# Top-k routing and experts of the last layer: ranking laid out over both halves of the partitions, and the chosen expert's product by masked features summed in PSUM

## The chip, the cores and the metric

The kernel runs on one core of one Trainium2 chip, as a single launch. The metric is the device time of that core in microseconds, as a median of several runs.

## The reference, cut to what matters

Four adaLN layers, each an attention and a feed-forward block, work on x of shape 8 x 256 x 128 in float32. The change lies in the last block alone: layer 3's mixture of 8 experts. With `h` the normalised and modulated x, and `gb` the block's gate vector per batch (sign times the larger of |g| and 0.25):

```python
# EPS = 1e-06, SINKHORN_ITERS = 8
t = jnp.log(jnp.clip(h @ gate_w, EPS))          # 8 batches x 256 tokens x 8 experts
for _ in range(8):
    t = t - logsumexp(t, axis=-2, keepdims=True)   # over the tokens
    t = t - logsumexp(t, axis=-1, keepdims=True)   # over the experts
gates = jnp.exp(t)
gv, idx = jax.lax.top_k(jnp.swapaxes(gates, -1, -2), m)   # m = 256 // 8 = 32 tokens for each expert
hard_gates = (gv > 0.5)
out = einsum(h[idx], experts) * hard_gates
y = zeros.at[idx].set(out)                      # .set: of several slots of a token, the last written stays
x = x + gb * y
```

So each of the 64 pairs of a batch and an expert takes its 32 best tokens. A token that several experts took gets the product of only one: the one with the latest slot, where the slot's order is rank first, then expert. For that the kernel needs each taken token's rank, and ties between equal gates are ordered by token, as top_k does.

## The kernel before, in words

x stays in SBUF as 16 tiles of 128 tokens x 128 dimensions (8 batches, 2 tiles each). Each engine has its own list of instructions, written out by hand in order, and engines meet only at semaphores. On DVE nearly every step of the routing goes through `then`, which makes the engine wait for the step's own completion before the next one. What runs in the last block, in order:

- `wide_front("l3_ffn")`: layer norm of all 16 tiles at once. DVE first copies silu(c) spread over 128 columns (L1838) for eight matmuls on PE (L991) that give the gate vector of each batch on all partitions. Then statistics, a power on POOL (L968), normalised tiles, transposes on PE (L997), scale and shift on ScalarE into `feats` (features of each batch, dimension on the partition, L3096), and the logits (L1003).
- `l3_ffn`: clip into `routes` (L2952), which also releases POOL's `partition_all_reduce` (L972). Then `wide_gates` on DVE (L1861 to L1867) makes the gate vectors, and then DVE waits for POOL's maximum (`sink_max`) ahead of L2973.
- `l3_route`: rescaling, then 8 rounds (`ROUNDS3`) of Sinkhorn without logarithms. Each is a sum over tokens by a matmul with ones on PE (L1689), and five small DVE steps (L2979 to L2983).
- Ranking: the gates are transposed to 64 partitions (batch and expert) x 256 tokens (L1693, L2989), three rows are filled (L2990 to L2992), and four rounds of MAX8 and MATCH_REPLACE8 give the 32 largest values in order (L2995, L2996). A loop over all 32 of them (L3001 to L3004) then runs four instructions for each value: how many of the top values a gate is below, where it equals the value, a running count of these, and a predicated copy of that count.
- The key (rank x 8 + expert) is transposed back (L1698) and seven small DVE steps (L3014 to L3020) leave a mask, tokens x experts, with a 1 for the winning expert.
- `l3_out`, once for each of 4 pairs of batches, in a hardware loop: PE multiplies a pair's features by all 8 experts (L1710, two halves of four matmuls of 128x512), and DVE adds the eight results of a tile, each weighted by its mask column (L3036, L3038: 64 instructions of 128x128 in a pair). Then DVE multiplies by the gate vector (L2754) and adds to x (L2756). PE's first half of the next pair waits for DVE's copy of the features, the second for x.
- SP waits for the last pair and stores all of x in one DMA of 1024 KB (L680).

Of the kernel before, what the change touches and what calls it, by code (L numbers as in the profile page):

```python
# [7 lines left out]
BF16 = mybir.dt.bfloat16  # L8
I32 = mybir.dt.int32
# [103 lines left out]
DVE_STEPS = {"l1_ffn": 4, "l2_ffn": 3, "l3_attn": 1, "l3_out": 36}  # L113
# [56 lines left out]
def adaln_program(nc, x_in, c_in, const_in, ali_in, weights_in, out):  # L170
    ctx = ExitStack()
    with ctx:
# [144 lines left out]
        best = sb("best", [P, T * B])  # L317
        ps = ctx.enter_context(nc.psum_tensor("bank", [P, 8, 512], F32))
# [86 lines left out]
        wide_silu = wide_signal("wide_silu", **dict.fromkeys(wide, 1))  # L405
        wide_mod = wide_signal("wide_mod", **dict.fromkeys(wide, 2))
# [8 lines left out]
        pair_ready = signal("pair_ready", l1_ffn=1, l2_ffn=1, l3_out=1)  # L415
# [14 lines left out]
        out_psum = signal("out_psum", l1_attn=1, l2_ffn=1, l3_attn=1)  # L430
# [41 lines left out]
        hid_ready = signal("hid_ready", l0_ffn=E0 * 2, l1_ffn=EA, l2_ffn=O2)  # L472
        silu_g = signal("silu_g", l1_ffn=EA)
        expert_psum = signal("expert_psum", l0_ffn=E0, l1_ffn=EA, l3_out=2)
# [11 lines left out]
        out_taken = signal("out_taken", l1_attn=1, l3_attn=1)  # L486
# [19 lines left out]
        routes_ready = once("routes_ready")  # L506
# [98 lines left out]
        def _(sp):  # L605
# [73 lines left out]
            sp.wait_ge(pass_done.sem, sum(PASSES.values()) + 1)  # L679
            sp.dma_start(out.rearrange("b (t p) d -> p (b t) d", p=P), x[:]).then_inc(stored, 16)  # L680
            sp.wait_ge(stored, 16)

        @block.gpsimd
        def _(pool):
# [270 lines left out]
            for ph in WEIGHED:  # L955
# [13 lines left out]
                if ph == "l3_ffn":  # L969

                    pool.wait_ge(routes_ready, 1)
                    nc.gpsimd.partition_all_reduce(colmax[:], routes[:].rearrange("p t b e -> p (t b e)"), P,  # L972
                                                   bass.bass_isa.ReduceOp.max).then_inc(sink_max, 1)


        @block.tensor
        def _(pe):
            mm = nc.tensor.matmul

            def wide_front(ph, logits):  # L980
# [4 lines left out]
                for j in range(2):  # L985
# [3 lines left out]
                pe.wait_ge(wide_silu.sem, wide_silu(ph, 0, 1))  # L989
                for b in range(B):  # L990
                    last = mm(pb[6 + b // 4][:, b % 4 * D:(b % 4 + 1) * D], silu_8[:, b, :], W(ph, "wmod")[:, 2 * D:3 * D],  # L991
                              start=True, stop=True)
                last.then_inc(wide_mod.sem, 1)
# [690 lines left out]
            def l3_route():  # L1684
# [7 lines left out]
                for t in range(T):  # L1692
                    last = nc.tensor.transpose(pb[1][0:B * E3, t * P:(t + 1) * P], routes[:, t].rearrange("p b e -> p (b e)"), C("ident"))  # L1693
                last.then_inc(sink_sum, 1)
                pe.wait_ge(sink_next, ROUNDS3 + 2)
                n = B * E3
                for t in range(T):
                    last = nc.tensor.transpose(pb[0][:, t * n:(t + 1) * n], qT[0:n, 2, t * P:(t + 1) * P], C("ident", n)[:, 0:n])  # L1698
                last.then_inc(sink_sum, 1)

            def l3_out(p, ph="l3_out"):

                pe.wait_ge(pair_ready.sem, pair_ready(ph, p, 1))
                for r in range(2):
                    if r:

                        pe.wait_ge(pass_done.sem, pass_done(ph, p, 1))
                    for t in range(T):
                        for j in range(2):
                            last = mm(pb[4 * r + 2 * t + j][:], pair_feat[:, (r * T + t) * P:(r * T + t + 1) * P],  # L1710
                                      W("l3_ffn", "experts")[:, j * 512:(j + 1) * 512], start=True, stop=True)
                    last.then_inc(expert_psum.sem, 1)
# [29 lines left out]
            with pe.Fori(0, PAIRS) as p:  # L1742
                l3_out(p)
# [3 lines left out]
        def _(dve):  # L1747
# [85 lines left out]
            def wide_front(ph):  # L1833
# [4 lines left out]
                V_.tensor_copy(silu_8, silu_c[:, layer * B:(layer + 1) * B].unsqueeze(2).to_broadcast([P, B, P])).then_inc(wide_silu.sem, 1)  # L1838
# [10 lines left out]
                V_.tensor_scalar(scale_8, pb[0][:, B:2 * B], 1.0, None, ALU.add).then_inc(wide_scaled.sem, 1)  # L1849
                dve.wait_ge(wide_rstd_ready.sem, wide_rstd_ready(ph, 0, 1))  # L1850
# [1098 lines left out]
            def l3_ffn(ph="l3_ffn"):  # L2949
# [4 lines left out]
                wide_gates(ph)  # L2954
# [3 lines left out]
            def l3_route():  # L2958
# [11 lines left out]
                over_e = lambda v: v.unsqueeze(2).to_broadcast([P, T * B, E3])  # L2970
                dve.wait_ge(routes_ready, 1)
# [5 lines left out]
                for r in range(ROUNDS3):  # L2977
                    dve.wait_ge(sink_sum, r + 1)
# [4 lines left out]
                    V_.tensor_tensor(rows, rows, over_e(best[:]), ALU.mult).then_inc(sink_next, 1)  # L2983

                R = B * E3
                gate, work, key, strict, seen, same, run, one = (qT[0:R, i, :] for i in range(8))
                top = small[9][0:R, 0:M3]
                dve.wait_ge(sink_sum, ROUNDS3 + 1)
                then(V_.tensor_copy(gate, pb[1][0:R, 0:S]))  # L2989
# [18 lines left out]
                then(V_.tensor_scalar(strict, strict, float(E3), -float(E3), ALU.mult, ALU.add))  # L3008
                V_.scalar_tensor_tensor(key, strict, C("expert1", R), same, ALU.add, ALU.mult).then_inc(sink_next, 1)
# [4 lines left out]
                then(V_.tensor_copy(masks3[:].rearrange("p t b e -> p (t b e)"), pb[0][:, 0:T * R]))  # L3014
                then(V_.tensor_reduce(best[:], keys, AX.X, ALU.max))
                then(V_.tensor_tensor(won, keys, over_e(best[:]), ALU.is_equal))
                then(V_.tensor_scalar(keys, keys, 0.0, None, ALU.is_gt))
                then(V_.tensor_tensor(won, won, keys, ALU.mult))
                then(V_.tensor_scalar(rows, rows, 0.5, None, ALU.is_gt))
                then(V_.tensor_tensor(keys, won, rows, ALU.mult))  # L3020

            def l3_out(p, following, ph="l3_out"):
                count[0] = 0
                dve.wait_ge(pass_done.sem, pass_done(ph, p, 1))
                step(V_.memset(gap[:], 0.0))
                chosen = small[0][:, 0:2 * T * E3].rearrange("p (t b e) -> p t b e", t=T, b=2)
                step(V_.tensor_copy(chosen, masks3[:, :, bass.ds(p * 2, 2), :]))
                settle(ph, p)
                for r in range(2):
                    dve.wait_ge(expert_psum.sem, expert_psum(ph, p, r + 1))  # L3030
# [549 lines left out]
```

## Time and profile before

| | us |
|---|---|
| median of 3 runs (2676.94 to 2680.75) | 2680.1 |
| the profiled execution's own time | 2681.6 |
| its span, first to last instruction | 2679.8 |
| PE busy in the span | 2004.3 (75%) |
| DVE busy | 1739.8 (65%) |
| ScalarE busy | 1144.0 (43%) |
| POOL busy | 880.6 (33%) |

The device time is the span and 1.8 us around it. The rows below are from the same profiled execution. Times are from the start of the span, so the last block is what lies after about 2489 us. "PEclk" is the clock that TensorE was granted, as a share of 2.4 GHz: 0.50 is the lower of its two levels, 1.2 GHz.

### The profile page before, as it was taken

The page shows a single profiled execution, that of the slowest core. Times are in us where ns is not written, and L with a number is a line of the kernel's source. Part 1 is how long each engine was busy: PE and PEld are TensorE (multiplying, and loading weights), DVE is VectorE, ACT ScalarE, POOL GpSimd, SP SyncE. Part 2 cuts the span into 40 slices and gives each one's busy share as a digit, 9 for nine tenths or more (in the row PEclk, how much of TensorE's full clock was granted, in tenths as well). Part 3 has the DMA queues.
Part 4 walks back from the last instruction along what each step waited for, and adds up shares of the span by engine and source line. Part 5 has one row for each costly group of instructions (what it writes and reads, how often), then busy time and mean ns, then how long its engine had stood idle before and what let it go on. Part 6 is the DMA issues. An engine that isn't in the chain of part 4 may idle for free.

```text
span 2679.8 us, 44272 instructions
## 1 busy us (share of the span) xinstructions
PE 2004.3 (75%) x14672; PEld 1405.8 (52%) x14672; DVE 1739.8 (65%) x5467; ACT 1144.0 (43%) x3362; POOL 880.6 (33%) x1155
## 2 busy tenths in 40 slices
PE   3878989964477766775769999957757999999405
PEld 2445666651356555564746666634433666666302
DVE  5777353245888888888656666657654666664597
ACT  1443333419677777776112222213422655656000
POOL 3433121033545765556500000024200555555000
PEclk9887889975555555555569999978967999999558
DMA  3111000020000000000010000011110000000000
GB/s 110 44 42 40 17 20 28 2 84 21 7 13 13 7 13 8 13 1 1 1 44 1 0 0 0 0 28 48 40 61 11 1 1 1 1 1 1 0 0 16
DMA packets 57761, 49.60 MB, mean 19 GB/s; under 512 B 7000, under 2 KB 55864, under 8 KB 57016
## 3 DMA queue, kind: packets, MB, share of 16 engines
q1 hardware_dynamic: 54500, 45.53, 5.3%
q10 hardware_dynamic: 3040, 1.38, 0.3%
q8 instruction: 107, 1.75, 0.3%
q14 instruction: 114, 0.93, 0.1%
HBM read 19.78 MB, written 1.05 MB: 8 GB/s over the span
## 4 chain that ended last, share of the span: by engine, by line
PE 42%; DVE 30%; issue 8%; ACT 8%; SPq 5%; POOL 5%; ACTq 1%; DMA 1%; DVEq 0%; POOLq 0%
PE bank L1526 5%; PE bank L1518 5%; PE bank L1519 5%; SPq L556 4%; DVE weights L2484 4%; PE bank L1595 3%; PE bank L1248 3%; ACT rope_c L3262 2%; ACT rope_s L3262 2%; PE bank L1264 2%; PE bank L1632 2%; PE bank L1644 2%; DVE small L2522 2%; DVE feat_o L2534 1%; POOL big L706 1%
## 5 line engine op out<-in xcount | busy, mean ns | idle before, releaser
L1432 PE MATMUL bank<-V,probsT 128*128 128x9 f32 x1024 | 236.1, 364 | 76.7 <-ACT probsT L3273 76.7
L1432 PEld LDWEIGHTS bank<-V,probsT 128*128 128x128 f32 x1024 | 226.2, 329 | 114.1 <-ACT probsT L3273 94.5
L2129 DVE TENSOR_REDUCE nmax<-bank 128x4 f32<-128x1024 f32 x144 | 176.1, 1223 | 81.3 <-PE bank L1064 81.2
L3328 ACT ACTIVATE hid<-bank 128x512 f32<-128x512 f32 x144 | 85.7, 597 | 283.7 <-PE bank L1519 272.6
L1526 PEld LDWEIGHTS bank<-weights,hid 128*128 128x128 f32 x1152 | 151.2, 193 | 78.7 <-issue 75.5
L2718 DVE TENSOR_TENSOR hid<-hid,bank 128x512 f32<-128x512 f32 x144 | 98.7, 688 | 127.6 <-PE bank L1526 123.4
L1526 PE MATMUL bank<-weights,hid 128*128 128x128 f32 x1152 | 152.5, 277 | 12.5 <-DVE hid L2718 10.1
L3273 ACT ACTIVATE probsT<-bank 128x512 f32<-128x512 f32 x128 | 76.0, 597 | 179.8 <-PE bank L1419 177.4
L1518 PE MATMUL bank<-O,weights 128*128 128x512 f32 x288 | 150.3, 604 | 2.6 <-DVE big L2658 2.6
L1519 PE MATMUL bank<-O,weights 128*128 128x512 f32 x288 | 148.9, 599 | 0.0
L2732 DVE SCALAR_TENSOR_TENSOR O<-bank,O 128x128 f32<-128x128 f32 x496 | 138.9, 343 | 0.0
L793 POOL MEMSET big<- 128x4096 bf16 x1 | 3.5, 3512 | 411.9 <-DVE x L2756 411.9
L2903 DVE TENSOR_TENSOR kT<-bank,weights 128x256 f32<-128x256 f32 x128 | 54.1, 422 | 123.0 <-PE bank L1595 122.9
L706 POOL TENSOR_TENSOR big<-big,rinv 128x512 f32<-128x512 f32 x128 | 131.6, 1049 | 4.0 <-DVE rinv L2896 4.0
L3362 ACT ACTIVATE big<-bank,nmax 128x256 f32<-128x256 f32 x256 | 118.4, 472 | 16.7 <-DVE nmax L2891 16.7
L3108 ACT ACTIVATE feat_o<-bank 128x1024 f32<-128x1024 f32 x72 | 73.7, 1023 | 114.1 <-PE bank L1090 84.5
L3108 ACT ACTIVATE O<-bank 128x1024 f32<-128x1024 f32 x72 | 73.7, 1023 | 112.7 <-PE bank L1090 84.9
L2411 DVE TENSOR_REDUCE nmax<-bank 128x2 f32<-128x512 f32 x128 | 84.9, 683 | 34.1 <-PE bank L1406 34.1
L1406 PE MATMUL bank<-qT 48*128 48x256 bf16 x256 | 70.7, 405 | 45.7 <-ACT weights L3216 33.3
L2891 DVE TENSOR_REDUCE nmax<-bank 128x2 f32<-128x512 f32 x128 | 82.3, 684 | 30.6 <-PE bank L1606 30.6
L1519 PEld LDWEIGHTS bank<-O,weights 128*128 128x128 f32 x288 | 55.7, 193 | 70.5 <-issue 70.5
L1632 PE MATMUL bank<-const,big 128*128 128x128 f32 x512 | 83.1, 285 | 12.2 <-POOL big L706 10.4
(622 smaller groups left out, 5564.7 us busy)
## 6 DMA issues: line engine op xcount, KB each, us to landing
qT<-parts SPq DMA_DIRECT2D x276, 32.0 KB
big<-V SPq DMA_DIRECT2D x192, 32.0 KB
big<-parts SPq DMA_DIRECT2D x180, 32.0 KB
weights<-in_weights_l_ffn SPq DMA_DIRECT2D x1, 4832.0 KB, 14.4
weights<-in_weights_l_attn SPq DMA_DIRECT2D x1, 3904.0 KB, 12.5
weights<-in_weights_l_ffn SPq DMA_DIRECT2D x1, 3628.0 KB, 12.8
qT<-V SPq DMA_DIRECT2D x96, 32.0 KB
weights<-in_weights_l_ffn SPq DMA_DIRECT2D x1, 2304.0 KB, 7.8
```

What stands on the lines that cost most here:

```text
L556: queue.dma_start(stacks[m % STACKS][to, u * HALF:(u + 1) * HALF], pair_of(m, at, *of)).then_inc(stack_in[u].sem, 16)
L706: nc.gpsimd.tensor_tensor(row, row, rinv[:, h % H, :].unsqueeze(2).to_broadcast([P, T, S]), ALU.mult).then_inc(scaled.sem, 1)
L1432: last = mm(pb[1][:, t * S + h * wide:t * S + (h + 1) * wide], probsT[:, h % 2, at:at + P], values_of(b, k)[:, h * wide:(h + 1) * wide], s ...
L1518: mm(pb[two][:], W(ph, "gate")[:, cols], pair_feat, start=True, stop=True)
L1519: mm(pb[two + 1][:], W(ph, "up")[:, cols], pair_feat, start=True, stop=True).then_inc(hid_psum.sem, 1)
L1526: last = mm(pb[6 + e % 2][:, j * D:(j + 1) * D], risen(e)[:, j * P:(j + 1) * P], W(ph, "down")[:, e * D:(e + 1) * D], start=True, stop=True)
L1632: last = nc.tensor.transpose(pb[3 + h % 2][:, k * S + t * P:k * S + (t + 1) * P], probs3[h % SLOTS3][:, t * S + k * P:t * S + (k + 1) * P] ...
L2129: V_.tensor_reduce(to, scored.rearrange("p (i a n) -> p i a n", i=HPG, n=n), AX.X, ALU.max, negate=True).then_inc(score_max.sem, 1)
L2484: link(V_.tensor_scalar(at_most[:, j, :], row_of(b, j), tried[at][:, 0, j:j + 1], 0.0, ALU.is_le, ALU.add, accum_out=tried[at][:, 1, j:j + ...
L2732: last = V_.scalar_tensor_tensor(pair_sum[:, j, :], down[:, j, :], w, pair_sum[:, j, :], ALU.mult, ALU.add)
L3108: nc.scalar.activation(turned_probs[n % TURNS], turned_scores, ACT.Exp).then_inc(turned_exp.sem, 1)
L3362: last = nc.scalar.activation(probs3[h % SLOTS3][:, t * S:(t + 1) * S], pb[h % 3][:, t * S:(t + 1) * S], ACT.Exp, bias=nmax[:, h % H, t:t ...
```

## The change

Six parts, all within the last block:

1. `wide_front` for this layer no longer spreads silu(c) and no longer runs the eight matmuls of L991. A third small matmul gives the gate as a column for each batch (dimension on the partition), and four tiny DVE instructions finish it while DVE waits for POOL's power. `wide_gates` is gone from `l3_ffn`.
2. The gates are transposed with each (batch, expert) row twice, on partitions 0 to 63 and 64 to 127 (`twice`). Each half then handles 16 of the 32 top values.
3. DVE's loop runs 8 times. The count "below how many values" is done for 8 values of each half on DVE, and for the other 8 on POOL (15 instructions of 128x256, into `above_pool`). The equal, scan and copy steps run only for values that occur more than once, at most 8 for each half (`classes`, found by seven small DVE steps).
4. The two halves' keys are added after the transposition back, and the winner becomes a number from 0 to 8 for each token instead of a mask.
5. `l3_out`: PE broadcasts the winner numbers to all partitions in PSUM (16 small bf16 matmuls). DVE writes eight copies of a pair's features, each zero where the token's winner is not that expert, and PE adds the eight products of a pair in one PSUM bank (`start=e == 0`, `stop=e == 7`). ScalarE multiplies by the gate column, PE transposes back, and DVE adds to x.
6. Each pair of batches is stored by its own DMA as soon as it is done.

```diff
+                    pool.wait_ge(routes_ready, 2)
+                    link(nc.gpsimd.tensor_scalar(above_pool, qT[:, 0, :], half_top[:, 0:1], None, ALU.is_lt))
+                    for m in range(1, M3 // 4):
+                        link(nc.gpsimd.tensor_scalar(above_one, qT[:, 0, :], half_top[:, m:m + 1], None, ALU.is_lt))
+                        link(nc.gpsimd.tensor_tensor(above_pool, above_pool, above_one, ALU.add))
+                    nc.gpsimd.memset(small[2][:, 0:1], 0.0).then_inc(above_ready, 1)
...
+            def l3_products(u):
+                for e in range(E3):
+                    pe.wait_ge(masked_ready.sem, masked_ready("l3_out", u, e + 1))
+                    mm(pb[OUT_BANKS3[u]][:], W("l3_ffn", "experts")[:, e * D:(e + 1) * D], masked[e], start=e == 0,
+                       stop=e == E3 - 1).then_inc(masked_used.sem, 1)
+            def l3_back(u):
+                pe.wait_ge(gated_ready.sem, gated_ready("l3_out", u, 1))
+                for j in range(2 * T):
+                    last = nc.tensor.transpose(pb[2 + u][:, j * P:(j + 1) * P], gated[u % 2][:, j * P:(j + 1) * P], C("ident"))
+                last.then_inc(rows_psum.sem, 1)
+            def l3_out():
+                pe.wait_ge(sink_next, ROUNDS3 + 3)
+                for u in range(PAIRS):
...
+                            last = mm(pb[2 + u][:, (i * T + t) * P:(i * T + t + 1) * P], winner[:, j:j + 1].to_broadcast([P, P]), identb[:],
+                                      start=True, stop=True)
+                    last.then_inc(sink_sum, 1)
+                l3_products(0)
+                for u in range(1, PAIRS):
+                    l3_products(u)
+                    l3_back(u - 1)
+                l3_back(PAIRS - 1)
...
-                V_.tensor_copy(silu_8, silu_c[:, layer * B:(layer + 1) * B].unsqueeze(2).to_broadcast([P, B, P])).then_inc(wide_silu.sem, 1)
+                if ph == "l3_ffn":
+                    wide_step_of(V_.memset(no_shift, 0.0))
...
-                wide_gates(ph)
...
                 for r in range(ROUNDS3):
+                    if r == 0:
+                        then(V_.memset(qT[:, 7, :], 1.0))
+                        then(V_.memset(qT[:, 3, :], 0.0))
...
+                    if r < ROUNDS3 - 1:
+                        V_.tensor_tensor(rows, rows, over_e(best[:]), ALU.mult).then_inc(sink_next, 1)
+                    else:
+                        for u in range(2):
+                            last = V_.tensor_tensor(twice_of[:, :, u].rearrange("p t (b e) -> p t b e", e=E3), routes[:], best_of, ALU.mult)
...
-                then(V_.memset(one, 1.0))
-                then(V_.memset(strict, 0.0))
-                then(V_.memset(seen, 0.0))
...
                     then(V_.max(top[:, 8 * i:8 * i + 8], src))
+                    if i == M3 // 8 - 1:
+                        for u, side in enumerate(sides):
+                            n[0] += 1
+                            V_.tensor_copy(half_top[side], top[side, u * M3 // 2:(u + 1) * M3 // 2]).then_inc(sink_step, 1)
+                        dve.wait_ge(sink_step, n[0])
+                        V_.memset(gap[:], 0.0).then_inc(routes_ready, 1)
...
-                for m in range(M3):
-                    v = top[:, m:m + 1]
-                    then(V_.scalar_tensor_tensor(strict, gate, v, strict, ALU.is_lt, ALU.add))
-                    then(V_.tensor_scalar(same, gate, v, None, ALU.is_equal))
+                then(V_.tensor_tensor(equal[:, 1:M3], top[:, 0:M3 - 1], top[:, 1:M3], ALU.is_equal))
+                then(V_.tensor_tensor(first_of[:, 0:M3], equal[:, 1:M3 + 1], equal[:, 0:M3], ALU.is_gt))
+                then(V_.copy_predicated(repeated, first_of.bitcast(I32), top))
+                then(V_.max(classes[:, 0:8], repeated))
+                then(V_.match_replace(repeated, classes[:, 0:8], repeated, -1.0))
+                then(V_.max(classes[:, 8:16], repeated))
+                then(V_.tensor_copy(classes[sides[1], 0:8], classes[sides[1], 8:16]))
+                for m in range(M3 // 4):
+                    j = M3 // 4 + m
+                    n[0] += 1
+                    V_.scalar_tensor_tensor(strict, gate, half_top[:, j:j + 1], strict, ALU.is_lt, ALU.add).then_inc(sink_step, 1)
+                    then(V_.tensor_scalar(same, gate, classes[:, m:m + 1], None, ALU.is_equal))
                     then(V_.tensor_tensor_scan(run, one, same, 0.0, ALU.mult, ALU.add))
                     then(V_.copy_predicated(seen, same.bitcast(I32), run))
                 then(V_.tensor_tensor(strict, strict, seen, ALU.add))
+                dve.wait_ge(above_ready, 1)
+                then(V_.tensor_tensor(strict, strict, above_pool, ALU.add))
...
+            def l3_masked(u):
+                dve.wait_ge(sink_sum, ROUNDS3 + 3 + u)
+                of_pair = feats[:, 2 * u:2 * u + 2, :].rearrange("p b k -> p (b k)")
+                for e in range(E3):
+                    if u:
+                        dve.wait_ge(masked_used.sem, masked_used("l3_out", u - 1, e + 1))
+                    V_.scalar_tensor_tensor(masked[e], pb[2 + u][:], e + 1.0, of_pair, ALU.is_equal, ALU.mult).then_inc(masked_ready.sem, 1)
+            def l3_add(u):
+                dve.wait_ge(rows_psum.sem, rows_psum("l3_out", u, 1))
...
+            def l3_out():
+                l3_masked(0)
+                l3_masked(1)
+                l3_masked(2)
+                l3_add(0)
+                l3_masked(3)
+                for u in range(1, PAIRS):
+                    l3_add(u)
...
+            def l3_gate(u):
+                act.wait_ge(masked_used.sem, masked_used("l3_out", u, E3))
...
+                    last = nc.scalar.activation(gated[u % 2][:, i * S:(i + 1) * S], pb[OUT_BANKS3[u]][:, i * S:(i + 1) * S], ACT.Identity,
+                                                bias=no_shift, scale=gates_col[:, 2 * u + i:2 * u + i + 1])
```

## Rows read from the trace of the kernel before

**Rows 1.** Windows: stretch, length, busy us by engine, PEclk, DMA share, GB/s.

```profile
2516.30:2540.50 24.20, 8.92 (x33) 7.42 (x34) 13.44 (x40) 0.00 (x0) 0.00 (x0) 0.50 0.00 0
...
2546.60:2613.00 66.40, 0.00 (x0) 0.00 (x0) 61.94 (x128) 0.00 (x0) 0.00 (x0) 0.50 0.00 0
2613.00:2680.00 67.00, 34.44 (x66) 13.74 (x66) 50.42 (x164) 0.00 (x0) 0.00 (x0) 0.83 0.06 16
...
2618.00:2621.00 3.00, 3.00 (x4) 1.42 (x5) 0.00 (x0) 0.00 (x0) 0.00 (x0) 0.50 0.00 0
...
2622.00:2649.00 27.00, 15.74 (x36) 6.06 (x34) 23.33 (x75) 0.00 (x0) 0.00 (x0) 0.99 0.00 0
```

**Rows 2.** Groups of instructions, 2546.6 to 2613.1: busy us, mean ns | idle before.

```profile
L3003 DVE TENSOR_TENSOR_SCAN qT<-qT 64x256 f32<-64x256 f32 x32 | 21.8, 682 | 1.1
L3001 DVE SCALAR_TENSOR_TENSOR qT<-qT,small 64x256 f32<-64x256 f32 x32 | 15.2, 476 | 1.1
```

**Rows 3.** Timeline of the norm and gates: start, us, instruction, idle before it.

```profile
2489.43 0.69 DVE L1838 COPY big<-silu_c 128x1024 f32<-128x1024 f32 x1
...
2497.66 4.19 DVE L1852 TENSOR_SCALAR big<-x,big 128x128 f32<-128x128 f32 x16 [2.88 <-POOL big L968]
...
2510.12 0.72 POOL L972 PARTITION_ALL_REDUCE colmax<-routes  x1 [12.50 <-DVE routes L2952]
...
2515.07 0.23 DVE L2973 TENSOR_TENSOR colsum<-colmax 128x64 f32<-128x64 f32 x1
```

**Rows 4.** Timeline, start of the ranking.

```profile
2541.67 0.27 DVE L2990 MEMSET qT<- 64x256 f32 x1
...
2542.74 0.42 DVE L2995 MAX8 small<-qT 64x8 f32<-64x256 f32 x1
```

**Rows 5.** Timeline, from the end of the routing to the last instruction.

```profile
2617.10 0.29 DVE L3020 TENSOR_TENSOR masks<-colmax,routes 128x128 f32<-128x128 f32 x1
...
2617.91 8.70 PE L1710 MATMUL bank<-weights,O 128*128 128x512 f32 x16 [2.67 <-DVE O L2704]
...
2673.53 0.69 DVE L2756 TENSOR_TENSOR x<-x,O 128x512 f32<-128x512 f32 x1
2674.25 0.41 SPq L680 DMA_DIRECT2D out<-x  x1
```

**Rows 6.** The output stage: groups of 2617.4 to 2680, and one timeline row.

```profile
L3038 DVE SCALAR_TENSOR_TENSOR O<-bank,small,O 128x128 f32<-128x128 f32 x112 | 34.1, 346 | 2.0
...
2629.10 3.70 PE L1710 MATMUL bank<-weights,O 128*128 128x512 f32 x8 [2.49 <-DVE O L1890]
```

**Rows 7.** Groups of POOL, whole span.

```profile
L714 POOL TENSOR_TENSOR qT<-kT 128x256 f32<-128x256 f32 x64 | 47.0, 734 | 48.1 <-DVE kT L2904 48.0
...
L860 POOL TENSOR_TENSOR hb<-hb,start_half 128x32 f32<-128x32 f32 x8 | 43.7, 5457 | 31.7 <-issue 31.6
...
L833 POOL CAST parts<-kT 128x512 bf16<-128x512 f32 x8 | 4.9, 616 | 0.5
...
L871 POOL TENSOR_SCALAR neg_mid<-neg_mid 128x32 f32<-128x32 f32 x8 | 2.4, 304 | 0.7
```

**Rows 8.** DVE beside a busy POOL: source view (min/median/max ns) and timeline at 2199.

```profile
L2912 DVE TENSOR_TENSOR sum_b<-sum_b,hid x8: 425/1272/1276, 2147.6 to 2488.4; 128x256 f32<-128x256 f32 x8
...
2199.15 2.22 POOL L706 TENSOR_TENSOR big<-big,rinv 128x512 f32<-128x512 f32 x2
2199.19 1.27 DVE L2912 TENSOR_TENSOR sum_b<-sum_b,hid 128x256 f32<-128x256 f32 x1
```

**Rows 9.** Nearest rows for the new instructions: groups of DVE and ScalarE, timeline at 1108.

```profile
L2718 DVE TENSOR_TENSOR hid<-hid,bank 128x512 f32<-128x512 f32 x144 | 98.7, 688 | 127.6 <-PE bank L1526 123.4 <-ACT hid L3328 2.9 <-issue 1.0
...
L2861 DVE SCALAR_TENSOR_TENSOR O<-bank,weights,big 64x512 f32<-64x512 f32 x4 | 3.0, 756 | 7.2 <-PE bank L1562 7.2
...
L3096 ACT ACTIVATE big<-bank,big 128x256 f32<-128x256 f32 x8 | 4.0, 560 | 16.0 <-PE bank L997 16.0
...
1108.11 0.19 DVE L2453 TENSOR_TENSOR small<-small 128x32 f32<-128x32 f32 x1
```

More of the change, by code:

```diff
@@ L317, in adaln_program @@
         best = sb("best", [P, T * B])
+        gates_col, mag_col, two_col = (small[1][:, i * B:(i + 1) * B] for i in range(3))
+        no_shift, numbers = small[1][:, 24:25], small[1][:, 32:32 + E3]
+        winner = small[0][:, 0:N16 // 2].bitcast(BF16)
+        masked = [rows(8 + 2 * e, 2) for e in range(E3)]
+        gated = [kT[:, 4 + 2 * i:6 + 2 * i, :].rearrange("p g n -> p (g n)") for i in range(2)]
+        OUT_BANKS3 = (6, 7, 0, 1)
+        half_top, equal, first_of, repeated, classes = (small[i][:, 0:n] for i, n in ((8, M3 // 2), (7, M3 + 1), (6, M3), (5, M3), (4, 16)))
+        side_rank = small[3][:, 0:1]
+        above_pool, above_one, twice = (kT[:, i, :] for i in range(3))
         ps = ctx.enter_context(nc.psum_tensor("bank", [P, 8, 512], F32))
@@ L984, in wide_front @@
                 layer = PHASES.index(ph) // 2
-                for j in range(2):
+                for j in range(3 if ph == "l3_ffn" else 2):
                     last = mm(pb[0][:, j * B:(j + 1) * B], W(ph, "wmod")[:, j * D:(j + 1) * D],
@@ L1741, in _ @@
             l3_route()
[L1742 to L1743 removed]
+            l3_out()
         @block.vector
@@ L2982, in l3_route @@
                     then(V_.reciprocal(best[:], rowsum3[:]))
-                    V_.tensor_tensor(rows, rows, over_e(best[:]), ALU.mult).then_inc(sink_next, 1)
+                    if r < ROUNDS3 - 1:
+                        V_.tensor_tensor(rows, rows, over_e(best[:]), ALU.mult).then_inc(sink_next, 1)
+                    else:
+                        for u in range(2):
+                            last = V_.tensor_tensor(twice_of[:, :, u].rearrange("p t (b e) -> p t b e", e=E3), routes[:], best_of, ALU.mult)
+                        last.then_inc(sink_next, 1)
                 R = B * E3
-                gate, work, key, strict, seen, same, run, one = (qT[0:R, i, :] for i in range(8))
-                top = small[9][0:R, 0:M3]
+                gate, work, key, strict, seen, same, run, one = (qT[:, i, :] for i in range(8))
+                sides = (slice(0, R), slice(R, 2 * R))
+                top = small[9][:, 0:M3]
                 dve.wait_ge(sink_sum, ROUNDS3 + 1)
-                then(V_.tensor_copy(gate, pb[1][0:R, 0:S]))
-                then(V_.memset(one, 1.0))
-                then(V_.memset(strict, 0.0))
-                then(V_.memset(seen, 0.0))
+                then(V_.tensor_copy(gate, pb[1][:, 0:S]))
                 src, other = gate, [work, key]
@@ L3016, in l3_route @@
                 then(V_.tensor_tensor(won, keys, over_e(best[:]), ALU.is_equal))
[L3017 to L3030, printed above, removed]
-                    for e in range(E3):
-                        for t in range(T):
-                            o = pb[4 * r + 2 * t + e // 4][:, e % 4 * D:(e % 4 + 1) * D]
-                            w, to = chosen[:, t, r, e:e + 1], pair_sum[:, r * T + t, :]
-                            if e == 0:
-                                step(V_.tensor_scalar(to, o, w, None, ALU.mult))
-                            else:
-                                step(V_.scalar_tensor_tensor(to, o, w, to, ALU.mult, ALU.add))
-                        settle(ph, p)
-                    if r == 0:
-                        dve.wait_ge(expert_psum.sem, expert_psum(ph, p, 2))
-                        step(V_.memset(gap[:], 0.0))
-                        if following is not None:
-                            take_pair(ph, following)
-                end_pair(ph, p)
@@ new lines, in l3_route @@
+                then(V_.scalar_tensor_tensor(won, keys, 0.0, won, ALU.is_gt, ALU.mult))
+                shared = won.rearrange("p (t b) e -> p t b e", t=T)
+                then(V_.scalar_tensor_tensor(shared, twice_of[:, :, 0].rearrange("p t (b e) -> p t b e", e=E3), 0.5, shared, ALU.is_gt, ALU.mult))
+                then(V_.tensor_tensor(won, won, numbers.unsqueeze(1).to_broadcast([P, N16, E3]), ALU.mult))
+                then(V_.tensor_reduce(best[:], won, AX.X, ALU.add))
+                V_.tensor_copy(winner, best[:]).then_inc(sink_next, 1)
@@ L3421, in _ @@
             wide_front("l3_ffn")
+            for u in range(PAIRS):
+                l3_gate(u)
 def shape_constants():
```

95 lines of the change are left out of this document (58 added, 37 removed).

## The prediction, made before the changed kernel had run

> **What bounds the kernel now.** The change touches only what lies after 2489 us, so I read the timeline and the windows there, and the kernel's averages not at all. The windows show one engine at a time at work. In the Sinkhorn rounds PE and DVE take turns (8.9 and 13.4 of 24.2 us) [rows 1]. In the ranking loop DVE is busy 61.9 of 66.4 us and no other engine has a single instruction [rows 1]. In the output stage DVE is busy 50.4 of 67 us [rows 1], while PE waits for it [rows 6]. So a microsecond taken from DVE's list here is a microsecond of the kernel, and one that is added is one too, unless DVE was waiting. I sum against the profiled execution (2681.6 us, of which 1.8 lie outside its span) and carry the difference over to the median of 2680.1.
>
> **The ranking loop: -50.7 us.** 32 passes take 66.4 us, 2.08 each [rows 1], for the four steps compare-and-add, compare, scan (0.68) and copy [rows 2]. The width is 256 columns before and after, and 128 partitions in place of 64 should cost DVE nothing. 8 passes remain. In each the first step (0.48) is no longer waited for, which I put at 0.1 less, so 8 x 1.98 = 15.8, against 66.5.
>
> **POOL beside it: +6.2 us, between 0 and +8.7.** POOL gets 8 compares and 7 additions of 128x256. An addition of that size takes 0.73 [rows 7]. The compare has no row: a one-input instruction takes 0.30 at 32 columns and 0.61 at 512, which gives 0.45 at 256 as an estimate [rows 7]. That is 8 x 0.45 + 7 x 0.73 = 8.7 us busy, and some 10 us with a gap of 0.1 after each. DVE has 0.5 + 1.6 + 15.8 + 0.5 = 18.4 us of its own between the release and the wait for `above_ready`, so POOL is done in time. But it isn't free: beside two POOL instructions of 1.1 us each, DVE's addition of 128x256 took 1.27 in place of its best 0.425, and 1.27 is its median over 8 [rows 8]. So DVE stood still for 0.85 of about 1.04 us, 82%. About 1.5 us of POOL's 8.7 lie beside DVE's MAX8 and MATCH_REPLACE8, with one input each, where I expect no loss. The rest: 7.2 x 0.82 = 5.9, rounded up for what the short steps lose. The ends are no collision at all and all of POOL's time.
>
> The trace shows that loss for an addition only. The Trainium skill ("SBUF — State Buffer", Who interferes with whom) says that a DVE instruction with two SBUF inputs, or in a two-port mode, shares a port with GpSimd under an exclusive lock. By it all four steps of the loop collide; were it only plain additions, this term would be near 1 us, and the sum 5 lower. The trace agrees with it where it shows anything [rows 8].
>
> **New short steps of the ranking: +1.9.** A step of 128x32 takes 0.19 [rows 9], and 0.22 with its wait. The seven steps that find repeated values: six x 0.22, and 0.3 for MATCH_REPLACE8 with its value load: 1.6. The two copies of 16 columns and the release: 0.35. Upper end: MAX8 at its 256-column price (0.42) for two of them, +0.5.
>
> **The fills: -1.1.** The three fills ahead of MAX8 took 2541.67 to 2542.74 [rows 4]. They and other small ones go into rounds 0 to 3, where DVE stands idle 24.2 - 13.4 = 10.8 us in 8 rounds, 1.3 each, most of it waiting for PE [rows 1]. The fullest round gets two fills of 0.38 and a tiny one, 0.86: hidden beneath PE's sum. Were it not, it would cost under 0.5 in all. The last round multiplies twice, +0.25.
>
> **After the loop: +1.5.** One more addition of 256 columns and one dearer combination: +0.6. Transposes of 128 in place of 64 columns, on both ways: +0.3. Adding the halves, and two more steps on 128x128 at 0.32 less what is fused: +0.6 to +0.7.
>
> **The gates and their silu: -0.5 and -2.5.** The copy L1838 (0.69) stood ahead of the statistics, and a tiny memset takes its place: -0.5, as the two overlapped a little [rows 3]. The eight PE matmuls lay under DVE's statistics: nothing. The four small gate instructions lie in DVE's wait of 2.88 us for POOL's power: nothing [rows 3]. `wide_gates` stood between the logits and the rounds, but POOL's all-reduce ran beneath it. The record gives this 0.72 us, ending at 2510.84, and DVE's next step started at 2515.07 [rows 3] without any wait. So the all-reduce really ended somewhere between. If the record is right, 4.1 us go; if it lasted the whole 4.9, none. POOL spans are called rough, so I take 2.5 and keep 0 and 4.1. The Trainium skill ("GPSIMD Engine Reference", Cross-partition — where GPSIMD wins) gives 247.7 us for a reduction over partitions of 2048 columns; in proportion an estimate for 128 would be 15.5, and my sum would rise by about 13. The row excludes it, for DVE would have waited.
>
> **The output stage: -22.2.** Before, from the end of L3020 (2617.39) to that of L2756 (2674.22): 56.8 us [rows 5]. Of it 34.1 are the 112 weighted additions [rows 6], which go. After, from the moment that the winners are ready:
> - 16 small bf16 matmuls of 128 columns, 0.15 each as an estimate from L1710 (0.43 for a record of 512 float32 columns at the full clock [rows 6]), end at 2.5. DVE's first masked tile needs only four of them and is ready at 1.4.
> - PE then has 32 products of 128x512. Each has two records, and 8 records took 3.70 at the full clock [rows 6], so 0.86 a product with its share of starting up; 16 took 8.70 while the clock rose [rows 5]. Before, the clock was 0.50 from PE's restart at 2617.91 to about 2621 and 0.99 after [rows 1, 5]. I take the same 3.3 us at half speed: half a product is done by then, 31.5 x 0.86 = 27.1 more.
> - DVE's masked tile (one PSUM and one SBUF input, 512 columns) costs 0.69 to 0.76 [rows 9], under 0.86, and POOL is idle. So PE is the bound and doesn't wait for DVE: eight buffers are filled again in the order in which PE frees them.
> - Two of the transposes back lie between products, 1.5 us together.
> - The end is a chain: two ScalarE instructions of 0.5 [rows 9], four transposes 0.9, the last addition 0.8 with its waits: 2.7.
>
> Sum 3.3 + 27.1 + 1.5 + 2.7 = 34.6, against 56.8. As low as 32, if transposes cost half, and as high as 38, if PE loses 0.1 for each product in waits.
>
> **The store: -2.6.** One DMA of 1024 KB took 5.6 us from its issue to the end of the span. The last of four carries a quarter. If about 2 of 5.6 are fixed and the rest goes by size, 3.0 remain. Between 0 and -4.
>
> **Sum.** -50.7 + 6.2 + 1.9 - 1.1 + 0.25 + 1.5 - 0.5 - 2.5 - 22.2 - 2.6 = -69.7. That is 2611.9 for the profiled execution and 2610.4 for the median: I say 2610.5.
>
> **Rivals.**
> - *PE stays at the lower clock in the products.* For: it had it for 3 us after the long pause of the ranking [rows 1]. Against: later in the same stage PE paused 2.49 us and more at a time and still had 0.99 over 27 us [rows 1, 6], and now it hardly pauses. The price is 31.5 x 0.86 = 27.1 more: 2637.6. 7%.
> - *POOL's part costs nothing*, since the instructions of the loop don't collide: 2604.3. For: only an addition is seen to collide. Against: 0.85 of 1.04 [rows 8]. It lies within my range. 12%.
> - *POOL becomes the bound and the kernel slower than before.* A compare may be as dear for each column as the power of L860, 5.46 us for 32 columns [rows 7], 0.17 each: 43.7 for 256, 349 for eight. It decides from about 1.5 us a compare, where POOL outlasts DVE's list, and eats the whole gain at about 10. At that price the time would be 2610 + 349 - 25, about 2934. Against: L871, a plain one-input instruction, costs 0.30 for the same 32 columns, and power is the only operation that is so dear. 2%.
> - *The masking makes DVE the bound of the output stage*, at over 0.86 for a tile: at 1.05, as if it ran behind each product's semaphore, 32 x 0.19 = 6 more: 2616.6. It lies in the range. 9%.
>
> **How the numbers follow.** The forecast's own case has 70%. The unknown terms (POOL +2.5 and -6.2, all-reduce +2.5 and -1.6, output stage +3.4 and -2.6, store +2.6 and -1.4, short steps +0.5) don't all fall one way: taken together as independent they are about +6 and -7. The range goes further, since several terms have no row of their own: 2600 to 2624. That leaves the half clock, the slow compare and a bit at each side outside. What a measurement can tell from no change is 0.2%, 5 us; the gain is 70, and nothing but the slow compare, or a hold-up that no row shows, brings it near. Faster 0.96, same 0.01, slower 0.03.
>
> **What would show it.** In the trace after: eight scans in the ranking loop, at about 0.68 if nothing collides and longer beside POOL; a stretch of some 25 us from the first MAX8 match to the end of the loop; L972's wait, now open to see ahead of the first rescaling; PE at 0.99 in the products with one record each 0.43 us; a gap of about 3 us from the last addition to the end of the span. I'm wrong if PE waits for masked tiles, if its clock stays at 0.50, if DVE waits for `above_ready`, or if the stretch from the last normalised tile to the first rescaling is no shorter than before.

## The result, and the profile after

The changed kernel takes 2596.0 us (median of 4 runs, 2594.6 to 2598.7), against 2680.4 for the kernel before beside it: a ratio of 0.9685, 95% interval 0.9668 to 0.9702. Measured again (r0 below), with more runs of before beside it, it was 0.9687 (0.9671 to 0.9703). I had forecast 2610.5, and 2600 to 2624. So the direction and most of the size were right, and the time lies 4 us below the range.

The spans of the two traces differ by 85.1 us. Cut at places that both have, and with what I had predicted for each piece (-44.5 is -50.7 and +6.2; my +1.5 for what follows the loop is split, as 0.1 of it falls ahead of the first MAX8):

| piece | before | after | measured | predicted |
|---|---|---|---|---|
| all that lies before the last block's norm | | | -8.1 | 0 |
| silu copy ahead of the statistics | 0.6 | 0.0 | -0.6 | -0.5 |
| statistics to first logits matmul | 12.8 | 12.7 | -0.1 | 0 |
| logits on PE | 6.8 | 3.8 | -3.0 | 0 |
| routes to the end of the first rescaling | 6.5 | 2.4 | -4.1 | -2.5 |
| to the first MAX8 (8 rounds, fills) | 26.5 | 25.7 | -0.9 | -0.75 |
| to the ranking loop | 3.9 | 6.1 | +2.2 | +1.9 |
| ranking loop | 66.5 | 20.1 | -46.5 | -44.5 |
| to the winners | 4.2 | 5.7 | +1.4 | +1.4 |
| output stage, to the last addition | 56.8 | 34.1 | -22.7 | -22.2 |
| to the end of the span | 5.6 | 2.8 | -2.8 | -2.6 |

The windows of after answer to [rows 1]: rounds, ranking loop, output stage, and the two parts of the latter by the clock.

```profile
2500.40:2524.80 24.40, 8.93 (x32) 7.42 (x32) 14.91 (x56) 0.00 (x0) 0.00 (x0) 0.50 0.00 0
2532.10:2552.20 20.10, 0.00 (x0) 0.00 (x0) 19.27 (x33) 0.00 (x0) 11.73 (x14) 0.50 0.00 0
2557.90:2594.70 36.80, 32.64 (x96) 15.88 (x96) 23.47 (x36) 4.09 (x8) 0.00 (x0) 0.92 0.10 29
2558.00:2561.90 3.90, 3.90 (x19) 2.68 (x19) 3.37 (x6) 0.00 (x0) 0.00 (x0) 0.50 0.00 0
2561.90:2592.00 30.10, 28.64 (x78) 13.10 (x76) 20.10 (x31) 4.09 (x8) 0.00 (x0) 0.99 0.08 22
```

PE is the bound of the output stage, 28.6 us busy in 30.1, as forecast, and its clock stays up. The groups of that stage show the other half of it: a masked tile costs DVE 687 ns, less than the 0.86 us from one product to the next, so DVE waits for PE and not the reverse (compare L3038 in [rows 6]).

```profile
L1721 PE MATMUL bank<-big,weights 128*128 128x512 f32 x64 | 29.3, 615 | 0.0
L3107 DVE SCALAR_TENSOR_TENSOR big<-bank,big 128x512 f32<-128x512 f32 x32 | 20.9, 687 | 3.5 <-PE bank L1721 2.6 <-PE bank L1736 0.7
```

The all-reduce can now be seen. In the timeline of after, DVE waits for it 0.96 us and goes on 0.10 us after the end of its record, which answers to [rows 3]: the record of 0.72 was right, and `wide_gates` had hidden nothing longer than that.

```profile
2497.95 0.29 DVE L2992 TENSOR_SCALAR routes<-bank 128x128 f32<-128x128 f32 x1 [4.73 <-PE bank L1021]
...
2498.38 0.73 POOL L983 PARTITION_ALL_REDUCE colmax<-routes  x1 [9.39 <-DVE routes L2992]
2499.21 0.23 DVE L3014 TENSOR_TENSOR colsum<-colmax 128x64 f32<-128x64 f32 x1 [0.96 <-POOL colmax L983]
```

The part that I had not looked at is the start of the kernel, 2.4 ms ahead of the change. POOL's timeline there, before and then after:

```profile
1.00 0.20 POOL L687 MEMSET future_t<- 128x128 bf16 x1
10.47 0.64 POOL L689 TENSOR_SCALAR_AFFINE_SELECT identb<-identb 128x128 bf16<-128x128 bf16 x1 [9.26 <-DVE small L1972]
```

```profile
0.99 0.20 POOL L698 MEMSET future_t<- 128x128 bf16 x1
1.69 0.29 POOL L700 TENSOR_SCALAR_AFFINE_SELECT identb<-identb 128x128 bf16<-128x128 bf16 x1 [0.49 <-POOL future_t L698]
```

The instruction's own semaphore wait is for three POOL memsets, done at 1.2 us in both, so the releaser named in the first (a DVE instruction) can't be what held it. Behind it hang two small DMAs and PE's first matmul, at 14.10 us before and 10.05 after. Up to 2078 us DVE's list is the same in both kernels, instruction for instruction, so one of its instructions can be followed. Here is the 201st, before and after:

```profile
152.93 0.42 DVE L2176 TENSOR_TENSOR sum_b<-bank,weights 128x256 f32<-128x256 f32 x1
```

```profile
148.33 0.42 DVE L2216 TENSOR_TENSOR sum_b<-bank,weights 128x256 f32<-128x256 f32 x1
```

### The profile page after: what moved, and what is told of

Same layout as the page of the kernel before. It is cut to its first block, busy times and chain, and to the rows that moved or that the text cites. A ratio compares the mean times of both kernels' runs of the same rounds, so it can differ in the third digit from the quotient of the medians.

```text
span 2594.7 us, 44049 instructions
## 1 busy us (share of the span) xinstructions
PE 1990.5 (77%) x14690; PEld 1394.5 (54%) x14690; DVE 1673.0 (64%) x5279; ACT 1148.5 (44%) x3370; POOL 894.2 (34%) x1171
## 4 chain that ended last, share of the span: by engine, by line
PE 44%; DVE 28%; ACT 8%; issue 7%; SPq 5%; POOL 5%; ACTq 1%; DMA 0%; DVEq 0%; POOLq 0%
PE bank L1544 5%; PE bank L1536 5%; PE bank L1537 5%; SPq L566 4%; DVE weights L2524 4%; PE bank L1613 3%; PE bank L1266 3%; ACT rope_c L3334 3%; ACT rope_s L3334 3%; PE bank L1282 3%; PE bank L1650 3%; PE bank L1662 2%; DVE small L2562 2%; DVE feat_o L2574 2%; POOL big L717 1%
## 5 line engine op out<-in xcount | busy, mean ns | idle before, releaser
L1544 PE MATMUL bank<-weights,hid 128*128 128x128 f32 x1152 | 152.5, 276 | 12.7 <-DVE hid L2758 10.3
L2451 DVE TENSOR_REDUCE nmax<-bank 128x2 f32<-128x512 f32 x128 | 84.9, 683 | 34.1 <-PE bank L1424 34.1
L725 POOL TENSOR_TENSOR kT<-kT 128x256 f32<-128x256 f32 x64 | 46.8, 731 | 137.4 <-DVE kT L2944 137.4
## 6 DMA issues: line engine op xcount, KB each, us to landing
weights<-in_weights_l_attn SPq DMA_DIRECT2D x1, 3904.0 KB, 12.7
```

Of the source, the lines that this page charges most:

```text
L1544: last = mm(pb[6 + e % 2][:, j * D:(j + 1) * D], risen(e)[:, j * P:(j + 1) * P], W(ph, "down")[:, e * D:(e + 1) * D], start=True, stop=True)
```

## The experiments

"Statistics to end" below is the stretch from the last block's first statistics to the end of the span: 189.8 us before, 113.3 after. It repeats to 0.3 us from trace to trace, while whole times of one kernel scatter by up to 13 us. Kernels e4, e5, e7 and e8 ran once each (2604.9, 2601.4, 2676.8 and 2592.6 us), so nothing is read from their whole times.

**The changed kernel again.**

> The changed kernel again, as the reference for the runs beside it. Its first trace was 85 us shorter than the trace of before, and only 77 of these lie behind 2489 us, where the change is. In the first 60 us POOL's first AFFINE_SELECT started at 1.69 us, against 10.47 before. Theory A (POOL's code): before ends with the code for the all-reduce loaded on POOL, so that the next execution has to load the ordinary code ahead of its first AFFINE_SELECT; after ends with ordinary POOL instructions, and the load falls into POOL's idle time. By A this run starts its AFFINE_SELECT near 1.7 us again. Theory B (chance of an execution): it may start anywhere between 1.7 and 10.5. The logits matmuls took 3.84 us against 6.84; if that is the phase of the clock and not the change, they may take either here. Time by both: 2594 to 2599.

Measured: 2595.5 us (2591.0 to 2603.2), AFFINE_SELECT at 1.69, statistics to end 113.1, logits 4.0. Its statistics began at 2488.3 us, in the first trace at 2481.4, with the same code: what lies upstream of the last block scatters by that much. Between the medians lie 82.0 us here and 84.4 in the first measurement. The last block makes 77.1 of them in the traces, which leaves 4.9 and 7.3 for all that lies upstream, and by the interval of the ratio here anything from 2 to 11.

**POOL's code at the start: before with one more instruction, after with a second all-reduce.**

```diff
 e1, before, behind the all-reduce
...
+                    nc.gpsimd.tensor_scalar(small[2][:, 0:8], small[2][:, 0:8], 1.0, None, ALU.mult)
 e2, after, behind POOL's counting
...
+                    pool.wait_ge(sink_next, ROUNDS3 + 3)
+                    nc.gpsimd.partition_all_reduce(colmax[:], routes[:].rearrange("p t b e -> p (t b e)"), P,
+                                                   bass.bass_isa.ReduceOp.max)
```

> The kernel before with one more POOL instruction at the end of its list: a 128x8 multiplication of an unused buffer behind the all-reduce, in which nothing waits for it. Theory A (POOL's code is carried from one execution to the next): the first AFFINE_SELECT starts near 1.7 us in place of 10.47, PE's first matmul near 10.0 in place of 14.1, and the time falls by 4 to 8 us. Theory B (chance): no change, within 2 us, and AFFINE_SELECT near 10.5 or scattered.

> The changed kernel with a second all-reduce on POOL, whose result nothing reads, issued when the winners are ready, so that it runs beside the output stage. Theory A: POOL ends with the all-reduce's code loaded, the next execution's first AFFINE_SELECT starts near 10.5 us again, and the time is 4 to 8 us above that of the changed kernel. Theory B: no change, within 2 us. If POOL's reads held DVE up in the output stage, at most 1 us more by either.

POOL's first AFFINE_SELECT in e1, and in e2:

```profile
1.70 0.29 POOL L689 TENSOR_SCALAR_AFFINE_SELECT identb<-identb 128x128 bf16<-128x128 bf16 x1 [0.49 <-POOL future_t L687]
```

```profile
10.18 0.28 POOL L700 TENSOR_SCALAR_AFFINE_SELECT identb<-identb 128x128 bf16<-128x128 bf16 x1 [8.97 <-issue]
```

Both start as theory A has it, and so do all twelve traces of this case: at 1.7 us where an ordinary POOL instruction follows the last all-reduce (nine traces), at 10.2 to 10.5 where none does (before, e2, e7). In e3 below, one instruction of 128x8 and a memset are all that is left behind it, and that is enough. PE's first matmul came at 10.42 in e1 and at 13.45 in e2. The trace of e1 also shows where the wait has gone. The added instruction waits for nothing, and yet it starts 7.67 us after the all-reduce:

```profile
2496.79 0.73 POOL L972 PARTITION_ALL_REDUCE colmax<-routes  x1 [12.49 <-DVE routes L2953]
2505.19 0.27 POOL L974 TENSOR_SCALAR small<-small 128x8 f32<-128x8 f32 x1 [7.67 <-issue]
```

How far the lead reaches is read from the 201st instruction of DVE: it started at 152.5, 152.9 and 153.8 us in the three traces with the late AFFINE_SELECT, and between 147.6 and 149.7 in the nine others, so about 4 us of the wait were still on the path there. Later the lead drowns in the scatter. At DVE's 1001st instruction the three stand at 667.0 to 674.3 and the nine at 663.7 to 672.1. The whole times resolve nothing: e1 2673.6 against 2677.5 for before (3.8 us less; the ratio, 0.9991 with 0.9978 to 1.0003, gives 2.4 and does not rule out no change), e2 2599.4 against 2595.5. Both have the sign of theory A and lie a little under the 4 to 8 us that it expected.

In the packed trace POOL's sequencer has two MODIFY_POOL_CONFIG instructions ahead of the all-reduce, two ahead of the next ordinary instruction where there is one, and two ahead of the first AFFINE_SELECT (at 1.42 us in before, 1.59 in after). That fits a change of code; that the wait is the loading of it is inferred. The Trainium skill ("GPSIMD Engine Reference", Instruction dispatch) gives about 6 us for the first call into freshly loaded code and says that no instruction in the profile shows it. From the first MODIFY_POOL_CONFIG behind the all-reduce to the instruction it took 7.7 us in e1, so the trace agrees in kind and is above it in size.

**Which clock the logits get.**

```diff
 e4, after: both lines of before kept, L991's matmuls and their silu copy, result not read
-                if ph != "l3_ffn":
-                    pe.wait_ge(wide_silu.sem, wide_silu(ph, 0, 1))
...
+                pe.wait_ge(wide_silu.sem, wide_silu(ph, 0, 1))
...
 e7, before: the same eight matmuls issued behind the logits
+                if ph == "l3_ffn":
+                    spread_gates()
```

> The changed kernel with the silu copy and the eight gate matmuls of before left in wide_front (their result is not read). In the two traces of before-like kernels (before, e1) the 32 logits records took 6.83 and 6.84 us, in four traces of after-like kernels 3.74 to 4.01, with all else up to there within 0.3 us. Theory L (the early matmuls decide which clock the logits get): logits at 6.8 us again and clock 0.50 in them, and the stretch from the statistics to the end 3.0 us longer, 116.2. Rival (where the block falls in time decides): logits at 3.7 to 4.0.

> The kernel before, with the eight gate matmuls of the last block issued behind the logits in place of ahead of the transposes. Theory L: the logits take 3.7 to 4.0 us in place of 6.84, at clock 1.0. Rival: 6.8 us. The gate matmuls themselves (1.7 to 3.5 us, by the clock) now stand between the logits and DVE's gate vectors, so that the whole stretch from statistics to end is 189.7 - 3.0 plus 1.5 to 3.5 by theory L, and 1.5 to 3.5 above 189.7 by the rival.

The logits' group in after, e4, e7 (mean ns of one record behind the bar):

```profile
L1021 PE MATMUL bank<-weights,big 128*128 128x8 f32 x32 | 3.8, 260 | 0.0
```

```profile
L1020 PE MATMUL bank<-weights,big 128*128 128x8 f32 x32 | 6.8, 357 | 0.0
```

```profile
L1007 PE MATMUL bank<-weights,big 128*128 128x8 f32 x32 | 4.1, 269 | 0.0
```

Theory L holds both ways. In the window of after the clock was 0.93 over the logits, in that of e4 0.50:

```profile
2494.00:2497.90 3.90, 3.90 (x34) 3.81 (x32) 0.00 (x0) 1.33 (x3) 0.00 (x0) 0.93 0.02 4
```

```profile
2499.80:2506.70 6.90, 6.86 (x34) 6.76 (x32) 0.01 (x1) 1.28 (x3) 0.00 (x0) 0.50 0.01 2
```

Over the transposes just ahead the clock was at the lower level in both (0.51 and 0.50). With the eight matmuls in place, PE's pause before these transposes was 5.9 us long in before, against 8.0 in after, and the logits stayed at the lower level throughout (6.8 us, three traces). Without them the level rose by the logits, in all nine traces that have it so (3.7 to 4.1 us). Statistics to end was 116.1 in e4 (116.2 expected) and 189.9 in e7, whose late matmuls gave the gain back (188.2 to 190.2 expected). So work that cost nothing where it stood cost 3.0 us later. Why these matmuls spoil a rise that comes several us later is not explained.

**POOL beside DVE.**

```diff
 e3, after: no counting on POOL
-                    link(nc.gpsimd.tensor_scalar(above_pool, qT[:, 0, :], half_top[:, 0:1], None, ALU.is_lt))
...
+                    nc.gpsimd.tensor_scalar(small[2][:, 8:16], small[2][:, 8:16], 1.0, None, ALU.mult)
...
-                    j = M3 // 4 + m
...
+                    for j in (2 * m, 2 * m + 1):
...
-                dve.wait_ge(above_ready, 1)
-                then(V_.tensor_tensor(strict, strict, above_pool, ALU.add))
 e8, after: POOL's additions replaced by compares
-                        link(nc.gpsimd.tensor_tensor(above_pool, above_pool, above_one, ALU.add))
+                        link(nc.gpsimd.tensor_scalar(above_one, qT[:, 0, :], half_top[:, m:m + 1], None, ALU.is_lt))
```

> The changed kernel without POOL's counting: DVE does all 16 compare-and-add steps of a half, and POOL keeps one tiny instruction behind the all-reduce. Collision theory (a POOL instruction keeps DVE's two-input steps waiting): the first four passes of the loop took 14.0 us against 8.0 for the last four... in the first trace the loop took 20.1 us where eight passes of 1.99 would be 15.9. So 4.2 us of waiting go, one addition of 0.46 goes, and 8 more steps at 0.4 to 0.5 come, 3.2 to 4.0: between 1.4 us faster and 0.6 slower than the changed kernel, so the same within 1.5 us. Rival (POOL's part is worth what it takes off DVE, no collision): 3 to 4 us slower than the changed kernel. All four loop steps should be at 0.48, 0.35, 0.69 and 0.44 in every pass.

> The changed kernel with POOL's seven additions replaced by seven more compares of the same size, so the counts of the first eight values of each half are left out and the output is not the reference's. In the first trace after, a compare takes 0.92 to 0.97 us and an addition 0.72 when nothing holds it. Theory (only POOL's instructions with two inputs keep DVE's two-input steps waiting): the ranking loop takes 16 to 17.5 us in place of 20.07. Rival (every POOL instruction does, as I predicted): 20 to 22 us. POOL's list lasts 15.5 to 17 us by both, so DVE doesn't wait for it.

(In the first of these the passes are miscounted: the first five took 14.1 us, the last three 6.0.) In e3 everything that POOL counted is left to DVE. Loop groups of after, and of e3:

```profile
L3075 DVE TENSOR_TENSOR_SCAN qT<-qT 128x256 f32<-128x256 f32 x8 | 6.7, 842 | 0.3
L988 POOL TENSOR_SCALAR kT<-qT,small 128x256 f32<-128x256 f32 x6 | 6.2, 1030 | 0.6
L989 POOL TENSOR_TENSOR kT<-kT 128x256 f32<-128x256 f32 x7 | 5.5, 783 | 0.6
```

```profile
L3070 DVE SCALAR_TENSOR_TENSOR qT<-qT,small 128x256 f32<-128x256 f32 x16 | 7.7, 484 | 0.6
L3074 DVE TENSOR_TENSOR_SCAN qT<-qT 128x256 f32<-128x256 f32 x8 | 5.5, 692 | 0.3
```

The collision is real: alone, the scan takes 692 ns, and 842 on average in after. But the loop took 20.06 us in e3 and 20.07 in after: POOL's share saves DVE in the loop exactly what it takes from it, and behind the loop it costs the addition of its result, 0.46. Statistics to end was 113.1 in e3 and 113.1 to 113.4 with the counting on POOL, the whole time 2598.3 (2594.3 to 2598.8) against 2595.5 (2591.0 to 2603.2): no difference in either.

In e8 the loop took 17.9 us, between what the two theories expected. No POOL instruction had two inputs there, and DVE still lost 2.0 us, so my "only two-input instructions" falls too. Thirteen compares ran beside that loop, which makes 0.15 us each as an estimate. By it the six compares beside after's loop cost some 0.9 of the 4.2 us, and the seven additions the other 3.3, or 0.47 each. The difference can be seen in single rows. First after, where a step of DVE begins just behind an addition; then e8, where a scan begins just behind a compare; then a step of 128x31 with two inputs within a compare of after:

```profile
2532.04 0.72 POOL L989 TENSOR_TENSOR kT<-kT 128x256 f32<-128x256 f32 x1
2532.08 0.96 DVE L3073 SCALAR_TENSOR_TENSOR qT<-qT,small 128x256 f32<-128x256 f32 x1
```

```profile
2534.23 0.92 POOL L988 TENSOR_SCALAR kT<-qT,small 128x256 f32<-128x256 f32 x1
2534.32 0.93 DVE L3075 TENSOR_TENSOR_SCAN qT<-qT 128x256 f32<-128x256 f32 x1
```

```profile
2530.01 0.94 POOL L986 TENSOR_SCALAR kT<-qT,small 128x256 f32<-128x256 f32 x1 [30.90 <-DVE gap L3058]
2530.45 0.19 DVE L3062 TENSOR_TENSOR small<-small 128x31 f32<-128x31 f32 x1
```

The first step took 0.96 us where it takes 0.48 alone, and ended 0.28 after the addition: that is how it would look if it had to wait for the addition's end. The scan lost only 0.24 of its 0.69 and ended 0.10 after the compare, and the small step took its usual 0.19. The Trainium skill's rule ("SBUF — State Buffer", Who interferes with whom) has a step with two SBUF inputs blocked for the whole of POOL's instruction. The addition's rows agree with it; the two beside a compare do not, as far as POOL's recorded spans can be trusted.

**The store.**

```diff
 e5, after
-            for u in range(PAIRS):
...
+            sp.wait_ge(pass_done.sem, pass_done("l3_out", PAIRS - 1, 2))
+            sp.dma_start(out.rearrange("b (t p) d -> p (b t) d", p=P), x[:]).then_inc(stored, 16)
...
```

> The changed kernel with the single store of before: one DMA of 1024 KB after the last addition. From the last addition to the end of the span 5.5 to 5.6 us, against 2.72 to 2.76 with four stores; the output stage before it unchanged at 34.0 to 34.4. Rival (the four stores slow the output stage or each other, so splitting gains less than the 2.8): the output stage gets shorter here by up to 1 us.

From the last addition to the end 5.53 us, the output stage 34.2: the split is worth 2.8 and costs nothing.

**The clock in the rounds and the output stage.** Since PE sits at 0.50 through all of the routing, I kept it busy.

```diff
 e6, after (e9: the same with FILL_ROUND = 0)
+FILL_ROUND, FILL_LOOP, FILL_LAST = 20, 100, 28
...
+            def warm(k):
+                for _ in range(k):
+                    mm(pb[7][:, 0:P], identb[:], identb[:], start=True, stop=True)
...
+                    warm(FILL_ROUND)
...
+                pe.wait_ge(above_ready, 1)
+                warm(FILL_LOOP)
...
+                warm(FILL_LAST)
```

> The changed kernel with idle matmuls on PE (bf16, 128 columns, result not read): 20 behind each round's sum, 100 during the last passes of the ranking loop, 28 before the winners. In the trace after, PE had clock 0.50 from the first round to 4 us into the output stage, and the two sums of a round took 1.11 us. Theory C (the clock is granted for PE's activity, and the sums and first products are slow for want of it): clock near 1.0 in the rounds, each round 0.4 to 0.5 us shorter (8 rounds: 25.65 to about 22.0 from the first rescaling to the first MAX8), the output stage 1.5 us shorter (34.0 to 32.5): 108 to 109 us from the statistics to the end, against 113.1 to 113.4. Rival (small matmuls don't raise the clock): the rounds as before or up to 0.6 us longer each, where the fillers run late at the lower clock: 113 to 118.

> The same with the fillers of the ranking loop and the winners alone, none in the rounds. Theory C: rounds unchanged (25.65), the output stage 1.5 us shorter, 111.5 to 112 us from the statistics to the end. Rival: 113.1 to 113.4.

The rounds' window in e6, for the first of after's above (25.65 by the same cuts):

```profile
2504.95:2527.57 22.62, 16.32 (x194) 14.82 (x194) 15.39 (x58) 0.00 (x0) 0.00 (x0) 0.91 0.00 1
```

The clock was 0.91, the rounds took 3.0 us less, and the output stage 32.6 (33.6 to 34.4 in the traces without fillers). Statistics to end was 108.5, and 111.5 in e9, whose rounds stayed at 0.50: both as theory C has it. That makes e6 the fastest last block of all, 4.8 us under after. Its whole time, 2594.1 (2588.2 to 2596.3; ratio to before 0.9682, 0.9666 to 0.9698), and e9's 2593.0 can't be told from after's 2595.5.

## Why the prediction was wrong, step by step

- *"The change touches only what lies after 2489 us."* This is the step that failed: it put at nothing, without a look, a piece that measured -8.1 in the two traces. The new POOL instructions behind the all-reduce move a wait of 8.5 to 8.8 us from the next execution's start to a place where POOL is idle. At the start some 4 us of it were on the path: e1 and e2 show this in both directions at PE's first matmul (3.7 us earlier, and 3.0 to 3.4 later), and the twelve traces show it up to 150 us. That it is in the whole time is likely and not resolved. The other 4 us I put down to scatter, whose cause is open. Its size can be seen: the statistics began between 2476.7 and 2490.0 us in the twelve traces, both ends in kernels with the routing of before. And e7, which has before's late start and the same instructions upstream, was 0.8 us behind before at 153 us and 4.5 ahead of it at 674.
- *"The eight PE matmuls lay under DVE's statistics: nothing."* This is the second term that was put at nothing, and it was wrong by 3.0 us. They were hidden where they stood, but set the clock of the logits: 6.8 us with them ahead, 3.7 to 4.1 without (e4, e7).
- *The all-reduce, -2.5.* Measured -4.1, the end of the range that I had given it. The profile's own row was right, and I had halved it.
- *The ranking loop, -50.7 and +6.2.* Eight passes alone would take 15.9 (15.8 predicted). The collision was +4.2. The reasoning from an addition's row to all of POOL's list was too coarse: a compare holds DVE far less than an addition. And my price of 0.45 for a compare was half of the measured 0.92 to 0.97. The two errors ran against each other, so that the term came out only 2.0 too high is luck in part.
- *Output stage, store, short steps, fills.* Within 0.5, 0.2, 0.3 and 0.2 us. The output stage went as reasoned: PE as the bound at 0.86 a product, a clock that rises once and stays, no wait for masked tiles. (The 0.86 is twice a record of 0.43; the row of 3.70 us for four products, from which I said it came, gives 0.93.) The rivals of a lower clock, of slow masking and of a slow compare didn't occur, and none of my four signs of being wrong appeared: the error lay where I had named none.
- *The range.* It added up only the errors of terms that I had. These came to about -4 together, which would have been 2606 and inside. The missed terms, 3.0 us, some 4 us and the scatter, all fell on the same side and carried the time below 2600.

## What to carry to other kernels

The last instruction of a helper engine can belong to the next execution's start: if POOL's list ends with an all-reduce, try one small ordinary instruction behind it, and look at the first 20 us of the trace. Work hidden under another engine can still be paid for through the clock of what PE does next, so ask of each matmul that goes or comes what PE runs after it. For small terms compare stretches between fixed points of the traces, since those repeat to 0.3 us where the whole times scatter by up to 13.

## What the runs showed of the hardware that I had not expected

- POOL's first AFFINE_SELECT started 8.5 to 8.8 us later in the traces of the three kernels whose last POOL instruction is an all-reduce. In e1 an instruction that waits for nothing started 7.67 us after the all-reduce.
- Eight matmuls that ended 10 us ahead decided whether a stretch of logits ran at the lower or the upper clock, 6.83 or 3.7 to 4.1 us.
- Small bf16 matmuls in PE's gaps brought the clock from 0.50 to 0.91 over the rounds, and the four matmul records of a round's sum from 1.12 to 0.66 us from the third round on.
- An offload of 13 us of POOL work beside a full DVE gained nothing: 20.07 us with it and 20.06 without. Beside DVE's steps an addition cost some 0.47 us and a compare of the same size some 0.15 (estimates from e3 and e8).
